# Query and key projections as seven block products, table and mixing work moved to GpSimd in the value stage

## What is computed

```python
W = weights[cond];  h = einsum('bct,bcd->bdt', x, W)     # mixes the 32 positions of a batch
q, k, v = h @ Wq + bq, h @ Wk + bk, h @ Wv + bv          # 512 -> 4096 = 32 heads x 128
q, k = rms_norm(q, gq), rms_norm(k, gk)                  # norm over all 4096
x = x + softmax(q k^T / sqrt(128)) v @ Wo + bo           # per batch and head, 32 x 32 scores
y = (causal convolution of x with K, + x * D) * mask     # K[h, l] = 2 Re sum_n Ct exp(dtA l), l < 512
out = x + y @ kernel + bias + sum_n gate_n (y A_n^T) B_n^T + (y As^T) Bs^T   # 16 low-rank pairs, rank 32
```

## Time and profile before

| | us |
|---|---|
| median of 3 runs | 927.58 (927.36 to 927.93) |
| profiled execution, its own time | 923.91 |
| its span, first to last instruction | 922.1 |
| TensorE, matmul busy | 900.1 |
| VectorE busy | 611.7 |
| ScalarE busy | 309.2 |
| GpSimd busy | 288.9 |

### The profile page before, as it was taken

The page is one execution under the profiler, slowest core; times in us unless marked ns, Lnnn a source line. Parts: engine busy times, 40 slices in busy tenths (PEclk is TensorE's granted clock), DMA queues, the critical chain, the costliest instruction groups (busy, mean ns, idle before and its releaser), DMA issues.

```text
span 922.1 us, 12726 instructions
## 1 busy us (share of the span) xinstructions
PE 900.1 (98%) x4753; PEld 748.8 (81%) x4753; DVE 611.7 (66%) x694; ACT 309.2 (34%) x450; POOL 288.9 (31%) x241
## 2 busy tenths in 40 slices
PE   6999999999999999999999999999999999999998
PEld 4888888888888888888778888888888888888465
DVE  4499999999897769955775645546365556442421
ACT  3334343333433354333352323313141423122400
POOL 1889999999990055006000000000000000100000
PEclk9999999999999999999999999999999999999999
DMA  9410111011111101272020010202020200910201
GB/s 210 105 47 23 45 45 45 23 45 45 46 45 45 45 23 45 58 151 61 1 92 1 25 68 0 91 0 91 0 91 0 91 0 31 386 61 26 46 35 57
DMA packets 82141, 54.10 MB, mean 59 GB/s; under 512 B 33582, under 2 KB 66702, under 8 KB 81958
## 3 DMA queue, kind: packets, MB, share of 16 engines
q1 hardware_dynamic: 81152, 53.32, 19.8%
q10 hardware_dynamic: 966, 0.48, 0.2%
HBM read 49.97 MB, written 3.82 MB: 58 GB/s over the span
## 4 chain that ended last, share of the span: by engine, by line
PE 89%; DVE 6%; issue 2%; ACT 1%; DMA 0%; DVEq 0%; ACTq 0%
PE psum L494 24%; PE psum L496 24%; PE psum L495 24%; PE psum L588 6%; PE psum L535 5%; PE psum L671 1%; DVE sumsq L970 1%; PE psum L514 1%; PE psum L700 1%; DVE w_lo L921 1%; PE psum L724 1%; DVE gated L988 1%; DVE scores L948 1%; DVE p_blocks L1082 1%; DVE qk_sb L961 0%
## 5 line engine op out<-in xcount | busy, mean ns | idle before, releaser
L494 PE MATMUL psum<-mix_hi,w_hi 128*128 128x512 f32 x512 | 202.6, 396 | 0.7 <-ACT params L769 0.5
L495 PE MATMUL psum<-mix_lo,w_hi 128*128 128x512 f32 x512 | 199.4, 389 | 0.0
L496 PE MATMUL psum<-mix_hi,w_lo 128*128 128x512 f32 x512 | 199.3, 389 | 0.0
L970 DVE TENSOR_TENSOR sumsq<-sumsq,sq 128x1024 f32<-128x1024 f32 x64 | 93.4, 1474 | 38.4 <-ACT sq L790 38.3
L1112 DVE TENSOR_TENSOR acc<-psum,acc 128x512 f32<-128x512 f32 x64 | 44.3, 692 | 111.6 <-PE psum L496 111.6
L494 PEld LDWEIGHTS psum<-mix_hi,w_hi 128*128 128x128 f32 x512 | 96.2, 188 | 20.8 <-DVE qk_sb L961 1.5
L475 POOL MEMSET ax<- 1x256 f32 x1 | 0.3, 307 | 359.4 <-DVE p_blocks L1082 359.4
L496 PEld LDWEIGHTS psum<-mix_hi,w_lo 128*128 128x128 f32 x512 | 96.1, 188 | 20.2
L495 PEld LDWEIGHTS psum<-mix_lo,w_hi 128*128 128x128 f32 x512 | 96.3, 188 | 18.8
L494 PE MATMUL psum<-wo_hi,attn_hi 128*128 128x512 f32 x256 | 100.2, 391 | 1.3 <-DVE wo_lo L1103 1.3
L494 PE MATMUL psum<-wv_hi,mix_hi 128*128 128x512 f32 x256 | 100.5, 393 | 0.8 <-ACT v_sb L827 0.8
(11 more groups left out here) (201 smaller groups left out, 1442.7 us busy)
## 6 DMA issues: line engine op xcount, KB each, us to landing
w_raw<-in_wq SPq DMA_DIRECT2D x32, 256.0 KB, 2.9
w_raw<-in_wk SPq DMA_DIRECT2D x32, 256.0 KB, 3.2
wv_raw<-in_wv SPq DMA_DIRECT2D x8, 1024.0 KB, 7.0
wo_raw<-in_wo SPq DMA_DIRECT2D x8, 1024.0 KB, 5.3
toep<-kpad_dram SPq DMA_DIRECT2D x2, 4096.0 KB, 14.0
x_nat<-in_x SPq DMA_DIRECT2D x4, 512.0 KB, 6.0
out_dram<-o_stage SPq DMA_DIRECT2D x8, 256.0 KB, 2.0
lb_nat<-in_lora_b SPq DMA_DIRECT2D x4, 256.0 KB, 7.0
```

What stands on the lines that cost most here:

```text
L494: mm(out, lh, rh, start=(n == 0), stop=False)
L495: mm(out, lh, rl, start=False, stop=False)
L496: last = mm(out, ll, rh, start=False, stop=(close and n == len(terms) - 1))
L970: v.tensor_tensor(sumsq[:, m, :], sumsq[:, m, :], sq[:, slot, m, :], ALU.add).then_inc(sum_ok, 1)
```

## The change

**Seven products.** Let q1, q2, k1, k2 be a head's weights, each over two of the four feature chunks, and b11, b12 (chunks 0 and 1), b21, b22 (chunks 2 and 3) the mixed x for the two halves of the tokens. Once, at the start, VectorE forms t1 = b12-b11, t3 = b22-b12, t2 = b22-t1 and b21-t2 in place in `mix_f`, a float32 copy of mix, and splits them into `t_hi`, `t_lo`. Per head GpSimd forms s1 = k1+k2, s3 = q1-k1, s2 = s1-q1, s4 = q2-s2 (`combine`; VectorE does it for heads 0 and 1). TensorE does p1 = q1 b11, p2 = q2 b21, p3 = s4 b22, p4 = k2 (b21-t2), p5 = s1 t1, p6 = s2 t2, p7 = s3 t3, 6 matmuls each, in the order p1, p2, p6, p5, p3, p7, scores of the head before, p4. ScalarE writes p1 plus bk to `qk_sb`; VectorE adds the others from PSUM onto it in seven operations of 512 columns (`post`: c11 = p1+p2, u2, u4, c12, c22, u3, c21). Squares are now taken from `qk_sb`, and the scaling by gq*gk and the extraction of the scores are ScalarE's. Seven blocks (q1, q2, k2, s1 to s4; 1792 columns) are split per head.

**Moved.** x goes by a 2 MB load into `acc` in the projection stage, GpSimd adds bo there. The first three exponentials stay; the range reduction goes to the first rounds of the value stage in chunks of 16 (the constant added at its end is prepared), the long exponentials become one Exp on ScalarE, and Tanh, Sin and Exp stand in round 1 before exp of the scores. K's matmuls stand before `attend(4)`. `mix_lora` is on GpSimd, A after the tables, B after K, both untransposed; VectorE transposes the sums in round 7. lora_a is loaded after `load_pair(2)`, lora_b after `load_pair(4)`.

**Memory and tail.** wv_raw, wo_raw and ffn_raw now share the place of their lo part, so a load of Wv waits for all value groups of the round before, one of Wo for all output groups. `toep0` is loaded in round 7, after the scratch writes of the mixed sums; toep is stored forwards and read backwards by the matmul, wo and acc are no longer reversed. Low-rank down products go in pairs (16 matmuls of 256 columns for 32 of 128), the feed-forward bias is added to `acc` by GpSimd.

```diff
+            sp.wait_ge(tlo_ok, 4)
+            sp.dma_start(acc[:], x_rows).then_inc(acc_in, 16)
...
+            def load_pair(t):
+                sp.wait_ge(v_mm, t * G + G)
+                load_v(t + 1)
+                sp.wait_ge(wo_mm, t * G)
+                load_o(t, wo_raw)
+            sp.wait_ge(p4_mm, HEADS - 1)
+            load_v(0)
+            sp.wait_ge(p4_mm, HEADS)
+            load_o(0, wo_raw)
+            sp.wait_ge(v_mm, G)
+            load_v(1)
...
+            sp.wait_ge(turned, 2)
             sp.dma_start(a_scr[:, :, :, RANK:].rearrange("p c g r -> p (c g) r"),
...
+                         a_turn[:].rearrange("p c g r -> p (c g) r")).then_inc(lora_out, 16)
...
             sp.wait_ge(soft, 6 * (NQ - 1) + 1)
...
+            sp.dma_start(toep0[:], bass.AP(kpad.tensor, 0, [[1, P], [PADL, 16], [1, 512]])).then_inc(toep_in0, 16)
...
+                pool.wait_ge(wlo_ok, h - 1)
+                pool.wait_ge(w_in[slot], count)
+                gp.tensor_tensor(part("s1"), part("k1"), part("k2"), ALU.add).then_inc(ws_ok, 1)
+                gp.tensor_tensor(part("s3"), part("q1"), part("k1"), ALU.subtract).then_inc(ws_ok, 1)
+                pool.wait_ge(ws_ok, h * 4 - 6)
+                gp.tensor_tensor(part("s2"), part("s1"), part("q1"), ALU.subtract).then_inc(ws_ok, 1)
+                pool.wait_ge(ws_ok, h * 4 - 5)
+                gp.tensor_tensor(part("s4"), part("q2"), part("s2"), ALU.subtract).then_inc(ws_ok, 1)
...
+            combine(4, 0, 96)
...
+            combine(5, 1, 96)
+            pool.wait_ge(bo_in, 16)
+            pool.wait_ge(acc_in, 16)
+            for n in range(2):
+                gp.tensor_tensor(acc[:, 4 * n:4 * n + 4, :], acc[:, 4 * n:4 * n + 4, :], repeat(bo_rows[:], 1, 4),
+                                 ALU.add).then_inc(acc_set, 1)
+                combine(6 + n, n, 128)
+            with pool.Fori(4, HEADS // 2) as i:
+                for j in range(2):
+                    combine(i * 2 + j, j, i * 32 + 32)
+            pool.wait_ge(p4_mm, HEADS)
+            pool.wait_ge(c21_ok, HEADS)
+            gp.memset(p_blocks[:], 0.0).then_inc(blocks_zero, 1)
...
+            step(gp.tensor_scalar(expo[:], expo[:], 88.0, -87.0, ALU.min, ALU.max))
             gp.memset(sm("t2"), 0.0).then_inc(ang_ok, 1)
...
+            pool.wait_ge(fn_ok, 3)
...
+            pool.wait_ge(soft, 6 * 2 + 1)
+            pool.wait_ge(la_in, 16 * 16)
+            mix_lora(0)
             pool.wait_ge(kern_ok, 1)
...
+            gp.tensor_tensor(k_sb[:, :, CL - 1], k_sb[:, :, CL - 1], d_rows[:], ALU.add).then_inc(kern_d, 1)
...
+            mix_lora(1)
...
+            for g in range(G):
+                pool.wait_ge(xt_mm, g + 1)
+                gp.tensor_tensor(acc[:, g, :], acc[:, g, :], fb_rows[:], ALU.add).then_inc(bias_ok, 1)
...
+                for i, c in enumerate(chunks):
+                    wh = w_hi[slot][:, W[block], HD * i:HD * i + HD]
+                    wl = w_lo[slot][:, W[block], HD * i:HD * i + HD]
+                    mm(bank(n), wh, hi[:, c, tok], start=(i == 0), stop=False)
+                    mm(bank(n), wh, lo[:, c, tok], start=False, stop=False)
+                    last = mm(bank(n), wl, hi[:, c, tok], start=False, stop=(i == 1))
+                return last
+            def p1(slot):
+                product(0, "q1", slot, mix_hi, mix_lo, K1, TOK1).then_inc(p1_mm, 1)
+            def p2(slot):
+                product(5, "q2", slot, mix_hi, mix_lo, K2, TOK1).then_inc(p2_mm, 1)
...
+            def head_qk(h, slot):
                 pe.wait_ge(wlo_ok, h + 1)
...
-                    for n in range(2):
-                        if not first:
-                            pe.wait_ge(free, h * 2 + (n - 1))
-                        elif m == 0:
-                            pe.wait_ge(mixlo_ok, 4 * n + 4)
-                        product3(bank(2 * m + n),
-                                 [(w_hi[:, slot, m, c, :], w_lo[:, slot, m, c, :],
-                                   mix_hi[:, c, HALF * n:HALF * n + HALF], mix_lo[:, c, HALF * n:HALF * n + HALF])
-                                  for c in range(KC)]).then_inc(done, 1)
-                        if m == 0 and n == 0 and not first:
-                            head_scores(h - 1, 1 - slot)
+                pe.wait_ge(p1_ok, h)
+                p1(slot)
+                pe.wait_ge(c11_ok, h)
+                p2(slot)
+                pe.wait_ge(c21_ok, h)
+                p6(slot)
+                pe.wait_ge(u4_ok, h)
+                p5(slot)
+                pe.wait_ge(c12_ok, h)
+                p3(slot)
+                pe.wait_ge(u3_ok, h)
+                p7(slot)
+                head_scores(h - 1, 1 - slot)
+                pe.wait_ge(u2_ok, h + 1)
+                p4(slot)
...
-            head_qk(0, 0, first=True)
...
+            pe.wait_ge(tab_ok, 1)
+            pe.wait_ge(v_ok, 5 * G)
+            for h in range(SEQ):
+                last = mm(bank(0, 1024)[0:CA, CL * h:CL * h + CL], u_tab[:, :, h], expo[:, 0:CL, h],
+                          start=True, stop=True)
+            last.then_inc(kern_mm, 1)
+            attend(4)
+            pe.wait_ge(kern_ok, 1)
...
+                src = bank(2 + g % 6).rearrange("p (c t) -> p c t", c=KC)
+                if g % 2 == 1:
+                    sc.activation(mix_f[:, :, tok], src, ACT.Copy)
+                sc.activation(mix_hi[:, :, tok], src, ACT.Copy).then_inc(mixhi_ok, 1)
+            for g in range(4):
+                mix_out(g)
+            act.wait_ge(ws_start, 4)
+            split_hi(0, 0, 7).then_inc(whi_ok, 2)
+            for g in range(4, G):
...
+            def extract(h):
+                act.wait_ge(s_mm, h + 1)
...
+                for b in range(BPG):
+                    src = bank(6, 1024)[quadrant(b), :].rearrange("p (g k) -> p g k", g=G)[:, :, quadrant(b)]
+                    last = sc.activation(dst[quadrant(b), :].rearrange("p (g k) -> p g k", g=G), src, ACT.Copy)
+                last.then_inc(s_ok, 1)
...
+                        act.wait_ge(ws_ok, h * 4)
+                        act.wait_ge(p4_mm, h)
+                    split_hi(1 - slot, 0, 4).then_inc(whi_ok, 1)
+                act.wait_ge(p1_mm, h + 1)
+                if not (isinstance(h, int) and h < 2):
+                    act.wait_ge(s_mm, h - 1)
+                sc.activation(qk_sb[:, slot, 1, halves(0)], bank(0), ACT.Identity, bias=bias("bk", h)).then_inc(p1_ok, 1)
+                if not last_head:
+                    split_hi(1 - slot, 4, 7).then_inc(whi_ok, 1)
+                if first:
+                    for n in range(4):
+                        t_hi_out(n)
+                else:
+                    square_k(h - 1, 1 - slot)
...
+                    if not (isinstance(h, int) and h < 2):
+                        act.wait_ge(q_sum, h - 1)
+                    sc.activation(sq[:, 0, :], qk_sb[:, slot, 0, :], ACT.Square).then_inc(q_sq, 1)
+                act.wait_ge(q_sq, h + 1)
+                at = here(h)
+                sc.activation(qk_sb[:, slot, 0, :], qk_sb[:, slot, 0, :], ACT.Copy,
+                              scale=gqk[:, bass.ds(at, 1)]).then_inc(q_ok, 1)
+                if not first:
...
+                if tables:
+                    act.wait_ge(ang_ok, 1)
+                    sc.activation(sm("thx"), sm("xr"), ACT.Tanh, scale=0.5).then_inc(fn_ok, 1)
+                    sc.activation(ang[:], ang[:], ACT.Sin).then_inc(fn_ok, 1)
+                    sc.activation(expo[:], expo[:], ACT.Exp).then_inc(fn_ok, 1)
...
-            def head(h, slot, first=False, last_head=False):
...
+                if n == "c11":
+                    dve.wait_ge(p1_ok, h + 1)
+                    dve.wait_ge(p2_mm, h + 1)
+                    v.scalar_tensor_tensor(q1, bank(5), dqk[:, bass.ds(h, 1)], k1, ALU.add, ALU.add).then_inc(c11_ok, 1)
...
+                if not first:
+                    post("c21", h - 1, 1 - slot)
+                    if not last_head:
+                        dve.wait_ge(p4_mm, h)
                 if not last_head:
-                    if not first:
-                        dve.wait_ge(k_mm, h * 2)
                     split_lo(h + 1, 1 - slot)
-                for n in range(2):
-                    tok = slice(HALF * n, HALF * n + HALF)
-                    dve.wait_ge(q_sq, h * 2 + n + 1)
-                    if n == 0 and not (isinstance(h, int) and h < 2):
-                        dve.wait_ge(s_mm, h - 1)
-                    v.tensor_scalar(qk_sb[:, slot, 0, tok], bank(n), params[:, PARAM["bq"], bass.ds(h, 1)],
-                                    gqk[:, bass.ds(h, 1)], ALU.add, ALU.mult).then_inc(q_ok, 1)
-                    if n == 0 and not first:
-                        extract(h - 1)
-                for m, done in enumerate((q_sq, k_sq)):
-                    if m == 1:
-                        dve.wait_ge(done, h * 2 + 2)
-                    if not first:
...
+                post("c11", h, slot)
```

(11 more changed lines are left out.)

692 lines of the change are left out of this document (395 added, 297 removed).

## The result

The changed kernel takes 949.11 us (median of 4 runs, 948.95 to 949.73) against 927.47 (4 runs, 924.21 to 927.93): a ratio of 1.0238, 95% interval 1.022 to 1.0256. It is slower by 2.4%; 924.0 was forecast, and 949.1 lies above the range of 908 to 944. The profiled execution took 949.06 for a span of 947.3, so against the profiled span of before, 922.1, there are 25.2 us to explain. The medians are only 21.6 apart. Over this and later rounds the kernel before ran between 923.8 and 924.2 us when its mean granted clock was 1.00, as in its profiled execution, and between 926.2 and 931.3 when it was 0.994 to 0.998, as in most; no trace shows where the clock fell there.

What follows compares the result with a forecast made beforehand. TensorE bound the old kernel; a ScalarE-VectorE ring would pace the new heads. Attention's -16.2 us plus 4.9, 3.5, 3.9 and 0.3 gave -3.6, applied to the 927.58 median: 924.0 us; range 914 to 935, with rivals 908 to 944.

Steps and rivals of the forecast that it cites:

- the ring: Projection heads: ScalarE and VectorE wait for each other in a circle that sets the pace, 11.77 us a head, not TensorE.
- ScalarE's part of the ring: Projection heads: ScalarE's w_hi and bias, 2.37 us, plus query square, scaled copy and score extraction, 3.36 us.
- The pace of a head: Projection stage: 11.77 us a head with handovers, 0.91 less than before; 11.4 to 12.7 as ends.
- The long-ring rival: Projection heads: GpSimd's combine blocks w_lo or the key sum in most heads, 12.3 us a head, 940 us; chance 0.25.
- The end without overlap: Projection heads: upper end of the pace, some 12.7 us a head if no consecutive instructions overlap.
- TensorE-bound rival: Projection heads: TensorE remains the bound at 11.31 us a head, 910 us in all; chance 0.22.
- GpSimd's combine at the start: First heads: late combine(4) and blocking by two long additions on acc cost 4.5 us together, bounds 0 and 13.
- The start: Start of the projection stage: products begin at 23.5 us and head 0 ends at 42.
- The last product: End of the projection stage: 42 + 31 x 11.77 + 4.5 = 411.4 us, against 431.54 before.
- The turn: From projections to attention: attention starts 35.8 us after the last product, at 447.2, 16.2 us earlier than before.
- Round 0: First round of the value stage: waiting for the next value weights' load and split costs +4.9 us, up to 7.5.
- Tables: Value stage, round 1: ScalarE's Tanh, Sin and Exp make value group 7 wait, +3.5 us (0 to 6).

## Why the prediction was wrong

The frame held: TensorE was not the bound of the new heads, the ring through w_lo, c11, u2, u4, the key sum, c12, the query square, the scaled copy, the copy-outs and w_hi was. That was the forecast's own mechanism, and three runs bear it out (two copy-outs, sums one column wide, w_lo behind c12). Two of its terms were sized wrong, ScalarE's part of the ring (5.73 us forecast, 6.36 measured) and the work of GpSimd in the first heads (4.5 forecast, 11.5 measured), and one cost was put at nothing, TensorE's lower clock around its idle stretches. Its terms, one by one:

- **The pace of a head.** VectorE's six terms: 6.00 forecast, 5.92 measured. ScalarE's part, 5.73 forecast, 6.36 measured, is the step that failed: "extraction 4 x 0.31" measured 1.54, since 0.37 us copies ran 0.38 apart with no overlap (+0.30); w_hi part one to bias 1.09 for 0.95 (+0.14); square to scaled copy 1.22 for 1.08 (+0.14). In the first two I carried the overlap of two w_hi in a row to pairs that don't have it; the third is a gap behind the square, of which 0.12 us went with constant addresses. With the rest that is 0.60 a head, 17.4 us over 29 heads. "Without any overlap some 12.7" was the upper end, and 12.37 is inside it.
- **The long-ring rival** (12.3, 940) had the size and not the mechanism: w_lo and the key sum were not blocked in steady heads, and taking GpSimd's sums away left 12.37. The end without overlap, 12.7, was the right rival, and had no chance of its own. The thresholds given with this rival are off, too: by the forecast's own slope of 30 us for 1 us of pace, the change is no longer faster by 0.2% from 11.83 and slower from 11.95, not from 11.95 and 12.08, so the forecast stood nearer to a loss than its chances say. (The TensorE-bound rival should read 908, not 910: 411.4 - 395.6 is 15.8.)
- **GpSimd's combine at the start.** 4.5 forecast, bounds 0 and 13. The wait at head 4 was named, with 68 against the measured 75.3. The first four heads lost 61.0 - 49.5 = 11.5 us against the steady pace, near the upper bound; spreading the work gave 9.2 back.
- **The start.** Products at 23.9 (23.5 forecast); head 0 ended at 43.9 (42), most of the difference being the clock, 0.53 from 36 to 40.
- **The last product** so came at 435.8 and not at 411.4, 24.4 late: 17.4 from ScalarE's part, 11.5 - 4.5 = 7.0 from the first heads, 1.9 from head 0, less 1.9 in the last two heads, for which I had taken the full ring though they need no further weights.
- **The turn.** 35.8 forecast, 40.15 measured. The idle stretch was foreseen (4.7; measured 5.1), the half clock behind it was not: 2.4. From the matmul that sums the squares to attention it took 25.4 us and not 23.9: the forecast had put GpSimd's blocking at nothing here, but beside its range reduction four operations of the norm and the softmax took 2.8 us more than before. Two of them, and the first of the two in the kernel before:
```profile
458.56 0.71 DVE L1300 TENSOR_SCALAR sm_s<-sm_s 128x256 f32<-128x256 f32 x1
...
461.09 2.06 DVE L1311 TENSOR_TENSOR sm_s<-scores,inv_norm 128x1024 f32<-128x1024 f32 x1
```
```profile
445.09 0.30 DVE L1051 TENSOR_SCALAR sm_s<-sm_s 128x256 f32<-128x256 f32 x1
```
- **Round 0.** +4.9 forecast; 53.98 against 51.23, +2.8. The load landed with attention's start (476.06) and not 2.6 behind it: in 5.4 us, not 7.0. (By the forecast's own numbers, 7.0 less 4.9, it would have been 2.1.)
- **Tables.** +3.5 forecast, +6.1 measured: the idle time at group 7 was 2.9 us, as worked out, and the half clock from 559 to 565 made 2.9 more. The tables were ready in time.
- **Kernel matmuls** +3.9, measured 3.9. **Mixing** 0, measured 0: rounds 2, 3, 5 and 6 took 50.68, though VectorE's operations were blocked. VectorE's groups in rounds 2 and 3:
```profile
L1270 DVE TENSOR_TENSOR wv_lo<-wv_raw,wv_hi 128x512 fp32r<-128x512 f32 x6 | 10.7, 1790 | 0.0
...
L1326 DVE TENSOR_TENSOR sm_s<-sm_s,row_inv 128x1024 f32<-128x1024 f32 x2 | 5.9, 2940 | 0.1
...
L1315 DVE TENSOR_REDUCE row_max<-sm_s 128x32 f32<-128x1024 f32 x2 | 2.4, 1220 | 0.1
```
Operations with two SBUF inputs took 1.79 instead of 0.68 and 2.94 instead of 1.23; the reduction with one, and the additions from PSUM, kept their durations. So the Trainium skill's rule on two SBUF inputs (SBUF — State Buffer, Who interferes with whom) agrees with the rows of the value stage, as it does with w_lo's 3.86 beside the long addition. One input is no safeguard for every operation: the scaling of 128x256 in the turn (L1300, above) has one, and took 0.71 instead of 0.30. In the steady ring w_lo and the key sum did not meet GpSimd's sums, as argued.
- **Tail** +0.3, measured -0.5.
- **From the profile to the median.** The terms above add up to 28.7 us, and the median is only 25.1 off. The forecast added to the changed kernel the 3.7 us by which the median of before lies above its profiled execution. In the changed kernel the two are alike (949.11 and 949.06), so 3.6 of the missing us were hidden by this addition, which is luck.

Of the signs listed ahead of the result, the ring showed itself as described (ScalarE without idle time up to w_hi, VectorE idle only before w_lo), and so did the gap of 3 us in round 1 and a wait for wv_raw (4.8 us for 4); w_lo took 2.09 us on average, under the 2.5 of the long ring. The pace, the last product and the start of attention did not come as listed. Neither sign of being wrong fired (head 0 ended before 46, rounds 2, 3, 5 and 6 took 50.68): none was set for a ring that is longer without being blocked. The ring was 5% short, and 29 heads multiplied it.

## What to carry to other kernels

When work moves off the bounding engine onto two others that wait for each other, walk the ring of waits once round and ask which instruction on it needs not stand there: here one line, w_lo behind c12, was worth 25 us, more than the 18 us for halving the copy-outs. Sum such a ring once with every overlap and once with none, and give both ends a chance of their own. Idle time on TensorE has a second price in the stretch behind it, so the gap of 5.1 us at the turn counted for 7.5.

## What the runs showed of the hardware

- TensorE's granted clock fell to its lower level, 1.2 GHz, with idle stretches of 2.04 us (the tail) to 7.3 us (the start), in part while TensorE still idled, and stayed there for 3 to 7 us: matmuls 0.43 apart instead of 0.227. Another idle stretch of 2.68 us left it at 2.4 GHz. Sixteen matmuls whose results nothing used kept it there through the turn. The one profiled execution of the kernel before does not show it; others of its executions had a mean clock of 0.994 to 0.998 and took 2 to 7.5 us longer.
- Consecutive ScalarE instructions overlap by 0.1 us in some pairs and not at all in others, with constant addresses as with computed ones. Four copies of 32x256 out of PSUM took 1.52 us.
- A VectorE operation with two SBUF inputs that starts during a GpSimd addition of 128x2048 (4.6 us) ends 1.9 us (w_lo, 3.86 us instead of 2.02) or 1.1 us (a sum of squares, 4.27 instead of 1.22) behind the addition, about its own duration; GpSimd's next sum, beside that w_lo, took 2.50 us instead of 0.73.
- A VectorE scaling of 128x256 with one SBUF input took 0.71 us beside GpSimd's range reduction and 0.30 in the kernel before.
- A GpSimd power of 128x32 took 5.47 us.
